# One wait per step on GpSimd between the gathers of the second and the third row

## The reference, cut to what matters

```python
loc = grid + kg + offsets            # offsets: a 3x3 convolution of the image, so the places depend on the data
loc = clip(loc, 0, W - 1)
x0, y0 = floor(x), floor(y);  x1, y1 = clip(x0 + 1), clip(y0 + 1)
def gather(yi, xi):
    idx = (yi * W + xi).reshape(B, -1, 1)
    v = jnp.take_along_axis(flat, idx, axis=1)
out = wa * gather(y0, x0) + wb * gather(y1, x0) + wc * gather(y0, x1) + wd * gather(y1, x1)
s = _conv_same(s, dw_w[g], dw_b[g], groups=Kin)   # depthwise 3x3 over the 9 * 32 sampled channels
s = _conv_same(s, pw_w[g], pw_b[g])               # 1x1 back to 32 channels
```

## Time and profile before

| | |
|---|---|
| median of 2 runs | 12362.09 us (12349.51 and 12374.67) |
| the profiled execution, span | 17350.5 us |
| the profiled execution, time around the span | none is given, so the span stands for it |
| instructions in the span | 102336 |
| GpSimd busy | 8759.5 us, 50% |
| TensorE busy | 8037.3 us, 46% |
| VectorE busy | 5165.4 us, 30% |

### The profile page before, as it was taken

The page is one execution under the profiler, slowest core; times in us unless marked ns, Lnnn a source line. Parts: engine busy times, 40 slices in busy tenths (PEclk is TensorE's granted clock), DMA queues, the critical chain, the costliest instruction groups (busy, mean ns, idle before and its releaser), DMA issues.

```text
span 17350.5 us, 102336 instructions
## 1 busy us (share of the span) xinstructions
PE 8037.3 (46%) x30934; PEld 5581.5 (32%) x30934; DVE 5165.4 (30%) x5993; ACT 1769.5 (10%) x2822; POOL 8759.5 (50%) x9300
## 2 busy tenths in 40 slices
PE   4444444445345544443335555344325555443358
PEld 2223223223234432232224443232223443222245
DVE  2222222322333233233222233223223223222323
ACT  1001101110000011100000001110000001110014
POOL 4555555455554555455554455555555444545530
PEclk7667677667667776666667777666667777666679
DMA  2222222222223321222123321222112332122233
GB/s 78 68 60 66 78 62 70 72 61 77 61 75 98 98 60 48 63 80 59 43 61 99 98 84 45 57 77 68 46 52 77 98 98 61 48 64 77 60 124 118
DMA packets 878203, 1254.74 MB, mean 72 GB/s; under 512 B 183384, under 2 KB 663064, under 8 KB 859992
## 3 DMA queue, kind: packets, MB, share of 16 engines
q0 software_dynamic: 294912, 604.57, 13.7%
q1 hardware_dynamic: 511784, 596.71, 10.7%
q10 hardware_dynamic: 71344, 51.39, 0.9%
HBM read 1069.42 MB, written 245.43 MB: 76 GB/s over the span
## 4 chain that ended last, share of the span: by engine, by line
another core or an unknown queue 40%; PE 20%; issue 19%; DVE 10%; ACT 3%; PEldq 2%; PEld 1%; SPq 1%; DMA 1%; ACTq 1%; DVEq 1%
PE acc L1307 8%; PE stage L1163 6%; DVE srow L1685 5%; PE stage L1035 2%; PEldq L483 2%; DVE gathered L1678 2%; PE pt L1294 1%; ACT stt L1008 1%; PEld acc L1307 1%; PE stage L1102 1%; PE stage L1081 1%; DMA off<-offs 1%; DVE wtn L1647 0%; SPq L694 0%
## 5 line engine op out<-in xcount | busy, mean ns | idle before, releaser
L543 POOL DMA_INDIRECT gathered<-table,idx x9216 | 8708.9, 945 | 7844.0 <-issue 4412.7
L1307 PE MATMUL acc<-stt,room 128*128 128x256 f32 (+2 forms) x15360 | 4368.5, 438 | 4763.0 <-ACT stt L1008 2491.7
L1307 PEld LDWEIGHTS acc<-stt,room 128*128 128x128 f32 (+1 forms) x15360 | 3242.4, 221 | 5803.8 <-issue 2728.6
L1685 DVE TENSOR_REDUCE srow<-gathered 128x576 f32<-128x2304 f32 x512 | 2097.1, 4096 | 324.7 <-remote 207.2
L1163 PE MATMUL stage<-room 128*128 128x128 f32 x6784 | 1035.3, 303 | 1067.5 <-issue 1049.5
L1163 PEld LDWEIGHTS stage<-room 128*128 128x128 f32 x6784 | 962.5, 218 | 1139.8 <-issue 1134.0
L1678 DVE TENSOR_TENSOR gathered<-gathered,wtb 128x2304 f32<-128x2304 f32 x512 | 1304.4, 2548 | 1.2 <-issue 1.2
L1008 ACT ACTIVATE stt<-pt 128x1024 f32<-128x1024 f32 (+1 forms) x512 | 415.6, 812 | 8375.5 <-remote 4988.2
L1666 DVE SCALAR_TENSOR_TENSOR xs<-acc,fused,xr 128x256 f32<-128x256 f32 x128 | 61.7, 482 | 3747.9 <-PE acc L1307 2206.0
L1035 PE MATMUL stage<-room,mat 128*128 128x512 f32 (+1 forms) x1360 | 776.2, 694 | 841.1 <-issue 338.9
L1294 PE MATMUL pt<-mat,srow 128*128 128x128 f32 x2048 | 427.2, 337 | 1475.6 <-DVE srow L1685 1250.7
(11 more groups left out here) (212 smaller groups left out, 4575.2 us busy)
## 6 DMA issues: line engine op xcount, KB each, us to landing
gathered<-table,idx POOLq DMA_INDIRECT x9216
room<-toep SPq DMA_DIRECT2D x48, 1792.0 KB, 7.0
room<-toep SPq DMA_DIRECT2D x64, 1280.0 KB, 8.0
room<-toep SPq DMA_DIRECT2D x64, 768.0 KB
table<-room SPq DMA_DIRECT2D x64, 512.0 KB
toep<-in_taps SPq DMA_DIRECT2D x128, 224.0 KB
gathered<-toep SPq DMA_DIRECT2D x16, 1792.0 KB, 7.0
toep<-in_taps SPq DMA_DIRECT2D x128, 160.0 KB
```

Source lines behind the costliest of these rows:

```text
L543: nc.gpsimd.indirect_dma_start(gat[r][:, k % K9 * G + k // K9, :], None, table[b].rearrange("(n e) -> n e", e=PAIR), bass.IndirectOffsetOn ...
L1307: ins = nc.tensor.matmul(sums_of[:, pairs, :], wk[0:kk, m, dx, at:at + P], stt[0:kk, slots, m, dx:dx + W], start=start and m == 0 and dx == 0,
L1685: nc.vector.tensor_reduce(srow[r % 2][:].rearrange("p (s c) -> p s c", c=CG), gat[r][:].rearrange("p s (q c) -> p s c q", q=4), AX.X, ALU. ...
```

## The change

GpSimd gets one more wait in each step. Ahead of the third row (r = 2) it waits until all 18 gathers of the second row (r = 1) of the same step have landed, and then goes on as before. Nothing else differs.

```diff
                 def step(n, b):
                     for r in range(ROWS):
                         v = n * ROWS + r
+                        if r == 2:
+                            pool.wait_ge(landed[1], 16 * GK * (n + 1))
                         pool.wait_ge(idx_given, v + 1)
                         pool.wait_ge(summed, v + 1)
                         pool.sem_inc(started, 1)
```

## The result

The changed kernel takes 12684.09 us (median of 2 runs, 12682.61 to 12685.57) against 12362.09: 322 us more, ratio 1.0263, 95% interval 1.0233 to 1.0293. It is slower by more than 2%. The forecast was 12620 us, 258 us more. In these runs, as in the experiments, the profiled execution is one of the timed ones (here the one of 12682.61 us).

A forecast was written before the change was run, and what follows sets the result against it. GpSimd's gather issue was taken as the limit, 72 x 1.248 = 89.9 us a step; landing 1.58 plus start 0.74 less normal gap 0.30 gave 2.02 us, times 128 = 258, so 12362 + 258 = 12620 us, range 12450 to 12700.

The forecast's parts named there:

- the sum: Whole kernel without stops, from the profile's pieces and the 1.248 us gather spacing: 12333 us against the timed median of 12362.
- something the profiler's presence adds: GpSimd's stops of 39.2 us a step in the profile, claimed to come from profiling and be absent in timed runs.
- A: Main forecast: GpSimd pays the stop before row three in full, 12620 us (12521 to 12654); chance 0.73.
- B: Rival: gathers cost less unprofiled, so GpSimd's idle time hides the wait and time stays about 12362 us; chance 0.13.
- C: Rival: pauses let TensorE catch up and give back more than they take, 12175 us; chance 0.06.
- the crawl: In the first profile, TensorE gets one matmul each 2.80 us while GpSimd issues, against 0.19 us with GpSimd stopped.
- The landing: Row two's transfer: VectorE starts 1.58 us (step 0 mean) behind the end of the last gather's instruction.
- D: Rival: large toep loads delay landings in 12 steps by some 6 us, 72 us more, 12692 us; chance 0.08.
- The start behind the release: GpSimd before row three: starts 0.74 us later after a release than another engine.
- the prediction's own sign: Idle time before row three's first gather about 2.3 us; prediction wrong if under 1.5 or over 2.6 us.
- the 2% mark: Time from which a measurement can tell the kernel from no change, 12609 us; A's middle lies just behind it.
- The price by the formula: Skill page's estimate for a gather: 2.15 us from its start, 1.21 behind the instruction's end; 211 us in all, 12573.

## Why the prediction was right, and where it was short

**What bounds the kernel.** Right, and it was the step on which all else hung. From a profile that was 4988 us too long it took only what was steady in it, the spacing of 1.248 us, and found that GpSimd never stops in the timed runs. The profile taken again shows exactly that. The 29 us that the sum lacked were no idle time either: there the gathers start 1.254 us apart (8748.4 / 9216 + 2805.8 / 9205), which is some 55 us more than the sum has for them, and what stands behind the last gather takes 626 us in place of 650. (The stops of 39.2 us "in each of the 128 steps" of that profile are a mean: they run from 0 to 65 us a step.) What was wrong is the words "something the profiler's presence adds": the eleven other profiles, of this kernel and its variants, have spans within 23 us of the median time of the same kernel. The same words gave the forecast of a span of 17100 to 17600 us, where it was 12680.8. It was that one execution, and why is open; only the one further profile of this kernel was taken.

**Nothing hides the stop (A against B).** Right. The table has time and stops equal within 15 us over a range of 0 to 1070 us.

**Faster (C).** Excluded: the crawl belonged to the one disturbed execution, and three pauses a step gave nothing back. That TensorE crawls because GpSimd issues was never in the rows: at 6047.60 it does 27 of the same matmuls in 3.33 us while GpSimd issues, and in the profile taken again GpSimd issues without a pause and TensorE is idle for 12.7 us before all of them, not 1067.5.

**The price.** 2.02 us a step was forecast, and 337 / 128 = 2.63 us measured in the trace. The two terms that make it up:

The landing, 1.58 us. In a quiet stretch it holds (1.65 and 1.54 us in the rows above). The step that failed is taking step 0's landing for all 128: where the band loads are under way it is 4.39 us in the step shown and 5.35 us at the most. That is rival (D), to which I gave 0.08. Its mechanism was right. Its size was near by luck: it has 12 steps of 6 us, 72 us, and the trace has 18 long stops in the stretches of these loads, each 3.1 us over the common one on average, 55 us. It isn't an alternative to (A) but a term of its sum, and I should have added it there: its rows were on the table, and 12692 would have been 8 us off.

The start behind the release, 0.74 us more than VectorE's. It was 0.87. Moving the wait showed that 0.10 of the missing 0.13 us are the two waits behind the added one, which I had named as queued behind it and priced at nothing; the other 0.03 are open. Over 128 steps the 0.13 us are 17 us.

258 + 55 + 17 = 330 us, against 322 and 334 measured in two comparisons; the rest up to the trace's 337 us is the three other long stops and a common landing of 1.60 in place of 1.58 us. The time lies in the range of 12450 to 12700 us, but above all that A alone allowed (12521 to 12654): it is the margin given for D that holds it, by 16 us. By the prediction's own sign the idle time before row three had to stay between 1.5 and 2.6 us. In the changed kernel its median is 2.46 us, but its mean is 2.93, and 21 stops are 3.5 to 6.2 us: that sign told of the missing term. The outcome, slower by over 2%, was the one held most likely, though only at 0.51: with the two missing terms the middle would have stood clear of the 2% mark.

**The price by the formula.** The Trainium skill, "DMA: Bandwidth & Descriptors", section "Anatomy of one DMA — SWDGE (gpsimd) path", gives 2.0 us plus the bytes at 436 GB/s for one DMA. With it the prediction had an estimate of 211 us (12573), which came out 111 us low. The runs don't agree with it for these gathers: in quiet steps they show 1.50 to 1.65 us between the end of a gather's instruction and VectorE's start on its landing, where the formula leaves an estimated 1.21, and it has no term for other loads under way.

No version here beats the kernel before. Apart from the smaller loads, which bring nothing, all of them only added to the engine that sets the time; the one gain found, the order of the waits, repairs a part of the change.

## What to carry to other kernels

A wait for one's own last transfer, on the engine that issues without a pause and sets the time, cost its full landing plus that engine's start here, each time: count it as landing + start - normal gap, and take the landing where other loads are in flight, not in a quiet stretch. If such a wait is needed, issue two transfers of the next group first; here that brought 322 us down to 62. And when a profile's span is far from the timed median, rebuild the time from the steady spacing of the busiest engine before believing any wait in it.

## What the runs showed that was not expected

A drain of GpSimd behind 18 gathers cost 6.86 - 0.30 = 6.56 us in step 1, and 865 / 128 = 6.8 us on average, where the wait for the landing of the same gathers costs 2.2 in quiet steps. What it does in the more than 4 us on top isn't known from these runs.

One profiled execution of the kernel before was 17350.5 us long, with TensorE, for some 40 us at a stretch, given one depthwise matmul each 2.80 us; the same kernel profiled again took 12365.4 us. A single profile can be a disturbed one even where the timed runs (12349.51 and 12374.67 us) agree.
